# Two heads' keys and queries in the two halves of the array's rows: a causal attention with a routed expert layer, one core

## What is computed

```python
q = (x @ Wq).reshape(B, S, HEADS, HEAD_DIM).transpose(0, 2, 1, 3)     # 16 heads of 16
c_kv = x @ Wkv_down
k = (c_kv @ Wk_up)...; v = (c_kv @ Wv_up)...
qf = concat(q_nope, rope(q_rope)); kf = concat(k_nope, rope(k_rope))
scores = jnp.einsum('bhqd,bhkd->bhqk', qf, kf) * scale
scores = jnp.where(causal, -jnp.inf, scores)
weights = jax.nn.softmax(scores, axis=-1)
out = jnp.einsum('bhqk,bhkd->bhqd', weights, v)
```

## Time and profile before

| | us |
|---|---|
| median of three runs | 789.13 |
| the profiled execution | 787.88 |
| its span, first to last instruction | 786.1 |
| TensorE (matmul) busy | 699.7 |
| VectorE busy | 567.3 |
| ScalarE busy | 397.4 |

### The profile page before, as it was taken

One profiled execution on the slowest core, in us unless ns is written; L12 is line 12 of the kernel. 1 busy time (PEld: TensorE's weight loads), 2 busy tenths in 40 slices (PEclk: granted clock), 3 DMA queues, 4 the chain that ended last, 5 costly groups with the idle time before them and its releaser, 6 DMA issues.

```text
span 786.1 us, 13117 instructions
## 1 busy us (share of the span) xinstructions
PE 699.7 (89%) x4086; PEld 444.5 (57%) x4087; DVE 567.3 (72%) x1297; ACT 397.4 (51%) x848; POOL 240.3 (31%) x297
## 2 busy tenths in 40 slices
PE   3579899899999999999999999999979999999910
PEld 3456575565665556556654555554467777777710
DVE  6666679778879977787698888863687755555545
ACT  2225365455656666667666776766823232222204
POOL 6526173440072207010611000010147413333332
PEclk9759899899999999999999999999999999999965
DMA  4864315035015101500341265332332223333254
GB/s 138 204 172 109 83 43 148 24 103 119 1 42 148 56 1 41 121 2 1 93 89 65 65 215 189 126 97 57 87 98 102 90 83 95 108 108 108 87 187 160
DMA packets 45096, 75.94 MB, mean 97 GB/s; under 512 B 5695, under 2 KB 23359, under 8 KB 44863
## 3 DMA queue, kind: packets, MB, share of 16 engines
q1 hardware_dynamic: 37423, 57.55, 27.2%
q0 software_dynamic: 4896, 13.67, 5.0%
q10 hardware_dynamic: 2720, 4.00, 1.4%
HBM read 41.91 MB, written 32.93 MB: 95 GB/s over the span
## 4 chain that ended last, share of the span: by engine, by line
PE 70%; DVE 16%; DMA 4%; issue 4%; ACT 3%; ACTq 1%; POOL 0%; SPq 0%; POOLq 0%; DVEq 0%
PE banks_ps L1144 15%; PE banks_ps L1124 14%; PE banks_ps L1085 14%; PE banks_ps L1181 7%; DVE mx L1342 6%; PE banks_ps L1215 5%; PE banks_ps L1001 3%; PE banks_ps L1092 2%; PE banks_ps L1194 2%; DMA q_stack<-m_rows 2%; PE banks_ps L1228 1%; ACT probs L888 1%; PE banks_ps L1277 1%; PE banks_ps L1203 1%; DVE base L1809 1%
## 5 line engine op out<-in xcount | busy, mean ns | idle before, releaser
L1342 DVE TENSOR_REDUCE mx<-banks_ps 128x1 f32<-128x512 f32 (+3 forms) x640 | 346.6, 602 | 93.1 <-PE banks_ps L1085 50.1
L888 ACT ACTIVATE probs<-banks_ps 128x512 f32<-128x512 f32 (+3 forms) x640 | 304.1, 546 | 180.9 <-PE banks_ps L1124 166.6
L1124 PE MATMUL banks_ps<-q_stack,k_stack 98*128 98x512 f32 (+3 forms) x640 | 244.9, 399 | 15.5 <-ACT probs L888 7.2
L1085 PE MATMUL banks_ps<-k_stack,q_stack 96*128 96x512 f32 (+3 forms) x640 | 237.0, 400 | 7.3 <-DMA q_stack<-kq_split 3.4
L1085 PEld LDWEIGHTS banks_ps<-k_stack,q_stack 96*128 96x128 f32 x640 | 124.8, 198 | 82.0 <-DVE mx L1342 37.1
L1124 PEld LDWEIGHTS banks_ps<-q_stack,k_stack 98*128 98x128 f32 x640 | 122.4, 195 | 51.4 <-ACT probs L888 29.1
L741 POOL TENSOR_SCALAR_AFFINE_SELECT probs<-probs 128x512 f32<-128x512 f32 x64 | 41.0, 640 | 331.0 <-ACT probs L888 331.0
L1144 PE MATMUL banks_ps<-probs,v_ones 128*17 128x512 f32 (+3 forms) x1280 | 134.1, 536 | 1.0 <-POOL probs L741 1.0
L798 POOL DMA_INDIRECT token_y<-ys,dest x47 | 45.4, 966 | 79.2 <-DVE ys L1785 76.3
L1144 PEld LDWEIGHTS banks_ps<-probs,v_ones 128*17 128x17 f32 x1280 | 29.5, 97 | 64.9 <-issue 41.1
L1181 PE MATMUL banks_ps<-w_up_sb,xg_t 128*128 x188 | 63.8, 462 | 0.3 <-ACT xg_t L941 0.3
(11 more groups left out here) (186 smaller groups left out, 685.0 us busy)
## 6 DMA issues: line engine op xcount, KB each, us to landing
kq_split<-kq_stage SPq DMA_DIRECT2D x32, 256.0 KB, 3.4
k_stack<-kq_split SPq DMA_DIRECT2D x8, 768.0 KB, 6.6
q_stack<-kq_split SPq DMA_DIRECT2D x32, 192.0 KB, 6.1
xg<-slot_x SPq DMA_DIRECT2D x47, 130.0 KB, 2.1
slot_x<-blank SPq DMA_DIRECT2D x11, 520.0 KB, 6.9
w_up_sb<-w_up SPq DMA_DIRECT2D x16, 352.0 KB
kq_split<-kq_stage SPq DMA_DIRECT2D x32, 128.0 KB, 3.2
x_raw<-xT SPq DMA_DIRECT2D x4, 512.0 KB, 5.7
```

The costliest lines, as they stand in the source:

```text
L888: nc.scalar.activation(probs[:, s % PROB_BUFS, h, off:CH], score_bank(n)[:, off:CH], ACT.Exp)\
L1085: ins = nc.tensor.matmul(dst[:, at:at + keys], q_stack[0:STACK, u % 4, h, tile * P:(tile + 1) * P], k_stack[0:STACK, pair, kb * CH + k0:kb ...
L1124: nc.tensor.matmul(score_bank(n)[:, off:CH], k_stack[:, 2 * g + h // 2, b * P:(b + 1) * P], q_stack[:, u % 4, h, off:CH], start=True, stop ...
L1342: last = nc.vector.tensor_reduce(mx[:, u % 2, h * TPC + tile, kb:kb + 1], bank_of(bank)[:, at:at + keys], AX.X, ALU.max)
```

## The change

The even head of a pair now has rows 0 to 47 of `k_stack` and `q_stack`, the odd one rows 64 to 111, with two rows of ones or of maxima behind each (48 and 49, 112 and 113). `q_stack` has one slot for a pair, and no zeros. A matmul then reads 48 or 50 rows of one half of the array's rows instead of 96 or 98. The program's matmuls on such operands carry a tile of 64 rows by 128 columns, at row 0 or row 64; all others keep 128 by 128, or 128 by 32 for the values.

A turn for maxima is now a pair of banks: two matmuls one behind the other, for the two heads, then two masks where there are masks, one wait before them and one release after VectorE's two reductions. The four scores of a step are issued in two twos, behind the pair of banks instead of between single banks. The rotation of the four PSUM banks hands two to each pair. Keys are loaded by two DMAs instead of one.

```diff
+ROWS = SPLIT + 2
+HALF_ROWS = P // 2
...
-        filled.append(filled[-1] + BANKS_A_STEP[u // UNITS_PER_CHUNK])
+        filled.append(filled[-1] + BANKS_A_STEP[u // UNITS_PER_CHUNK] / 2)
...
     for n, turn in enumerate(turns):
-        bank = n % TURN_BANKS if n < first_alone else LAST_MAX_BANKS + n % 2
-        turn_bank[turn], turn_before[turn] = bank, user.get(bank)
-        user[bank] = turn
+        wide = 2 if turn in max_no else 1
+        turn_banks[turn] = [(at + k) % TURN_BANKS if n < first_alone else LAST_MAX_BANKS + at % 2 for k in range(wide)]
+        turn_before[turn] = [user.get(bank) for bank in turn_banks[turn]]
+        user.update((bank, turn) for bank in turn_banks[turn])
+        at += wide
...
-                    sp.dma_start(k_stack[0:STACK, 4 * m:4 * m + 4, c * CH:(c + 1) * CH].bitcast(F32),
-                                 kq_dram[c, n - 1].rearrange("two copy (d j) n -> (two copy d) j n", j=GH)).then_inc(k_stacked, 16)
+                    for par in range(2):
+                        sp.dma_start(k_stack[half_rows(par, SPLIT), 4 * m:4 * m + 4, c * CH:(c + 1) * CH].bitcast(F32),
+                                     kq_dram[c, n - 1, par].rearrange("copy (d j) n -> (copy d) j n", j=GH)).then_inc(k_stacked, 16)
...
                 for tile, k0, keys, at in parts:
-                    ins = nc.tensor.matmul(dst[:, at:at + keys], q_stack[0:STACK, u % 4, h, tile * P:(tile + 1) * P],
-                                           k_stack[0:STACK, pair, kb * CH + k0:kb * CH + k0 + keys],
+                    for par in range(2):
+                        ins = nc.tensor.matmul(bank_of(of, par)[:, at:at + keys],
+                                               q_stack[half_rows(par, SPLIT), u % 4, pair, tile * P:(tile + 1) * P],
+                                               k_stack[half_rows(par, SPLIT), stacked, kb * CH + k0:kb * CH + k0 + keys],
...
-                nc.tensor.matmul(score_bank(n)[:, off:CH], k_stack[:, 2 * g + h // 2, b * P:(b + 1) * P],
-                                 q_stack[:, u % 4, h, off:CH], start=True, stop=True).then_inc(pe_scores, 1)
+                nc.tensor.matmul(score_bank(n)[:, off:CH], k_stack[half_rows(h % 2), 2 * g + h // 2, b * P:(b + 1) * P],
+                                 q_stack[half_rows(h % 2), u % 4, h // 2, off:CH], start=True, stop=True).then_inc(pe_scores, 1)
...
                 for half in range(2):
-                    for h in (2 * half, 2 * half + 1):
-                        run_banks(banks[h])
-                        if s < NS:
-                            score_head(s, h)
+                    run_banks(banks[half])
+                    if s < NS:
+                        score_head(s, 2 * half)
+                        score_head(s, 2 * half + 1)
...
-            nc.vector.memset(q_stack[0:STACK, 2:4].bitcast(F32), 0.0).then_inc(zeros_high, 1)
...
+                for tile, _, keys, at in bank_parts(of):
+                    for par in range(2):
+                        n = mx_row_of(pair, par, tile)
+                        last = nc.vector.tensor_reduce(mx[:, u % 2, n, kb:kb + 1], bank_of(of, par)[:, at:at + keys], AX.X, ALU.max)
+                last.then_inc(max_done, 1)
```

More of the change, by code:

```diff
@@ L80, in build_program, with max_pairs, bank_parts @@
     first_step[UNITS] = len(steps)
-    def max_banks(u):
+    def max_pairs(u):
         c = u // UNITS_PER_CHUNK
-        return [(u, h, i, kb) for h in range(GH) for i in range(TPC) for kb in range(c)] + \
-               [(u, h, n, c) for h in range(GH) for n in range(len(OWN_BANKS))]
-    def bank_parts(bank):
-        u, h, n, kb = bank
+        return [(u, pair, i, kb) for pair in range(GH // 2) for i in range(TPC) for kb in range(c)] + \
+               [(u, pair, n, c) for pair in range(GH // 2) for n in range(len(OWN_BANKS))]
+    def bank_parts(pair_of_banks):
+        u, pair, n, kb = pair_of_banks
         if kb < u // UNITS_PER_CHUNK:
@@ L118, in build_program @@
         at = min(at, first_step[u] - MAX_AHEAD)
-        for bank in reversed(max_banks(u)):
+        for bank in reversed(max_pairs(u)):
             while at >= 0 and len(max_at[at]) >= room(at):
@@ L489, in score_bank, with bank_of, half_rows, mx_row_of @@
             return turn_ps[:, k - SCORE_BANKS]
-        def bank_of(turn):
-            return turn_ps[:, turn_bank[turn]]
+        def bank_of(turn, k=0):
+            return turn_ps[:, turn_banks[turn][k]]
+        def half_rows(par, rows=ROWS):
+            return slice(HALF_ROWS * par, HALF_ROWS * par + rows)
+        def mx_row_of(pair, par, tile):
+            return (par * (GH // 2) + pair) * TPC + tile
         def wait_read(eng, job):
@@ L960, in bank_free @@
             def bank_free(turn):
-                before = turn_before[turn]
-                if before in max_no:
-                    pe.wait_ge(max_done, max_no[before])
-                elif before:
-                    wait_read(pe, before)
+                for before in turn_before[turn]:
+                    if before in max_no:
+                        pe.wait_ge(max_done, max_no[before])
+                    elif before:
+                        wait_read(pe, before)
                 return bank_of(turn)
@@ L1331, in _, with reduce_pair @@
                                         ALU.subtract).then_inc(w_ready, 1)
-            def reduce_bank(bank):
-                u, h, i, kb = bank
-                c = u // UNITS_PER_CHUNK
-                n = max_no[bank]
-                if u >= 2 and bank == max_banks(u)[0]:
-                    dve.wait_ge(mx_ready, u - 1)
-                dve.wait_ge(pe_max, n)
-                for tile, _, keys, at in bank_parts(bank):
-                    last = nc.vector.tensor_reduce(mx[:, u % 2, h * TPC + tile, kb:kb + 1],
-                                                   bank_of(bank)[:, at:at + keys], AX.X, ALU.max)
+            def reduce_pair(of):
+                u, pair, i, kb = of
+                if u >= 2 and of == max_pairs(u)[0]:
+                    dve.wait_ge(mx_ready, u - 1)
+                dve.wait_ge(pe_max, max_no[of])
+                for tile, _, keys, at in bank_parts(of):
+                    for par in range(2):
+                        n = mx_row_of(pair, par, tile)
+                        last = nc.vector.tensor_reduce(mx[:, u % 2, n, kb:kb + 1], bank_of(of, par)[:, at:at + keys], AX.X, ALU.max)
                 last.then_inc(max_done, 1)
@@ L1669, in _ @@
             for s in range(NS + 1):
-                banks, jobs = quarters(max_at[s]), quarters(aux_at[s], 2)
-                for k in range(4):
-                    for bank in banks[k]:
-                        reduce_bank(bank)
-                    if k % 2:
-                        for job in jobs[k // 2]:
-                            if job in by_dve:
-                                read_aux(job)
-                    norm_part(s, k)
+                banks, jobs = quarters(max_at[s], 2), quarters(aux_at[s], 2)
+                for half in range(2):
+                    for bank in banks[half]:
+                        reduce_pair(bank)
+                    norm_part(s, 2 * half)
+                    for job in jobs[half]:
+                        if job in by_dve:
+                            read_aux(job)
+                    norm_part(s, 2 * half + 1)
                 for u in range(UNITS):
```

71 lines of the change are left out of this document (35 added, 36 removed).

## The result

The changed kernel takes 883.43 us (median of 4 runs, 881.68 to 884.77) where the kernel before takes 789.62 on the same chip (4 runs, 788.01 to 790.67): 1.1189 times, 95% interval 1.116 to 1.1217. The forecast was 782, with 0.36 on slower. Its profiled span is 883.0 us against 786.1. The ratios of this document leave out executions more than 1.5% above the fastest of their kernel, so where the times scatter a ratio is not that of the two medians.

What follows compares the result with a forecast made beforehand. TensorE's issue was taken as a narrow bound, VectorE next. Full steps -7, side jobs -9 and +6, own banks +2, start +2, last unit -1 sum to -7 us: 787.9 to 781 profiled, 782 median; range 762 to 806.

Steps and rivals of the forecast that it cites:

- What bounds the kernel: Before the change, TensorE's issue bounds full steps narrowly (5.72 of 5.76 us for two steps); VectorE is next.
- the chain of full steps: Off-diagonal steps with maxima: the wait moves to the two-pair buffer before VectorE; 0.17 us less per two steps, -7 us.
- Overlap of the halves: Two 512-column matmuls side by side in the array's halves take 0.24 us; bounds 0.235 (full overlap) and 0.47 (none).
- Rival C: No overlap: matmuls in two halves follow one another, a two costs 0.47 us; +18, 806 us; chance 0.12.
- Side jobs: 128 by 128 jobs beside maxima: odd steps absorb 0.5 us each, -9 us; even steps pay 0.2 each, +6 us.
- rival A: Tiling changes cost 0.6 us or more, not 0.4; pairs needing the pair just before idle VectorE; 800 us; chance 0.28.
- Own banks: Own banks and diagonal steps, bounded by TensorE: islands cost 0.4 us each, twos save 0.24; +2 us, bounds -10 to +30.
- the island: Mask at 128 rows between 64-row matmuls: tiling change out and back plus two weight loads, some 0.4 us.
- The start: Unit 0: queries load 0.5 us late, own pairs with masks make TensorE slower than VectorE by some 1.5 us; +2 us.
- A: In "A's price", rival A; in "idle gaps is A", the experiments' theory that the clock falls because TensorE works less of the time.
- the spoiler: Granted clock under 1.00 in units 8 to 15, the array being asked for less; no size or chance given.
- TensorE's busy time falls by tens of us: Sign that the forecast is right: TensorE's busy time falls by tens of us while the span hardly moves.

Runs made afterwards that it cites:

- run 2: Changed kernel with its pair order kept, but keys and queries stacked at full height (96 and 98 rows, zeros) as before: 847.73 us, 1.0605 times the kernel before.
- run 12: The changed kernel measured once more, nothing edited, beside the later experiments: 884.92 us, 1.1231 times the kernel before.
- run 3: Changed kernel with its half-height layout kept, but banks and scores issued singly in turns as before: 943.2 us, 1.1797 times the kernel before.
- run 10: Kernel before with only its operand rows edited, maxima and scores both over rows 0 to 63: 951.71 us, 1.2057 times the kernel before.

## Why the prediction was wrong

**What bounds the kernel; the chain of full steps: right.** 5.59 us was forecast for two full steps, 5.68 came: right in kind, but half of the forecast gain (0.08 us where 0.17 was added up). In the chain, pair 4 was to start 3.15 us after pair 1 and started 3.18 after; the next block was due at 3.75 and came at 3.84 (0.03 of the 0.09 is there already, and 0.07 is the way from the pair to its scores, 592.38 to 592.69, where 0.24 was counted; the way into the values, 0.35, is as forecast). TensorE's gain went into a wait for the two-pair buffer, as said: its weight loads wait 71.6 us for VectorE, 37.1 before.

**Overlap of the halves: right, at the upper bound.** 0.24 for a two. Rival C fell on this (its mark was blocks over 5.9); run 2 shows what it would have been: 6.34.

**Side jobs: wrong in sign at the full clock.** -3 us was forecast for all of them, with 0.5 gained wherever a job stands in an odd step. Seven of the 21 periods at the full clock have a side job beside maxima; each got longer, together from 45.42 to 48.90 us. In the second trace of the changed kernel (run 12) there are five, from 31.11 to 33.31. The period that starts at 357.59 us before and 425.65 after has two jobs and grew from 6.87 to 7.57: the pair behind the first job starts at 430.67, after an idle gap of 0.55 that VectorE ends, 3.18 after the first pair (427.49). That is when the second pair is reduced, not the first. The job had taken one of the four banks, so the pair behind it needed banks of the pair just before. This is a mechanism of rival A, which the sum left out.

**Own banks: right.** In the changed kernel:

```profile
435.07 0.50 PE L1096 MATMUL banks_ps<-k_stack,q_stack 48*128 48x512 f32 x2
435.50 0.28 PE L1105 MATMUL banks_ps<-mask_b,ident_b 128*128 128x128 bf16 x2
435.72 0.50 PE L1137 MATMUL banks_ps<-q_stack,k_stack 50*128 50x512 f32 x2
436.06 0.40 PE L1096 MATMUL banks_ps<-k_stack,q_stack 48*128 48x384 f32 x4
...
438.59 0.38 PE L1096 MATMUL banks_ps<-k_stack,q_stack 48*128 48x256 f32 x2 [0.53 <-DVE mx L1354]
```

From 435.07 to 436.06 are 0.99 us for a pair of own banks, two masks and two scores: 0.48 for the twos, 0.08 for the masks at the 0.04 of the earlier trace rows, so 0.43 for the island, where 0.4 was taken. The wait of 0.53 at 438.59 stands behind a side job, as above. Five periods at the full clock have own banks and no job; together they fell from 31.42 to 30.73 us (four in run 12, from 26.38 to 25.22).

**The start: right.** The first exponential starts at 54.2 us where it started at 52.7, 1.5 later; +2 was forecast.

**What the sum would have been at the full clock.** The four periods of full steps alone went from 23.54 to 24.02 us (run 12: 23.34 to 23.03), those of the last unit from 25.69 to 25.11. The 78 periods are 33 with jobs beside maxima, 13 with own banks alone, 24 of full steps and 8 of the last unit. With the change of each kind as the two traces give it, the stage would be 8 to 17 us longer at the full clock (an estimate; periods of one kind differ among themselves), nearly all by the side jobs: some 797 to 806 us, near rival A, and not 782. A's price in the prediction is itself not added up well: 782 and +15 to +30 have their middle at 804, not 800.

**The step that failed: the clock.** The prediction used the full clock for every duration of units 8 to 15, and its last sentence named the spoiler, "A granted clock under 1.00 in units 8 to 15 would spoil all of it, since the array is asked for less", without a price, a rival or a chance. It happened, in 57 of 78 periods. So the sign "TensorE's busy time falls by tens of us" came out the other way: it rose from 699.7 to 757.8 us, since the same matmuls took longer. The price can be read from one period that holds the same work in every kernel and is at the low level throughout or nearly so: 5.52 us in the kernel before at the full clock, 7.08 in the changed kernel, 7.83 in run 3, 9.58 in run 10. Overlap makes the low clock cheaper, but not free. Over the stage +96.0 us stand against 255.8 - 17.7 = 238.1 us more low clock, 0.40 us for each; without the 8 to 17 us of above it is 0.33 to 0.37, so 79 to 88 of the 96 us are the clock's (an estimate). The reason given in the prediction was also only half of it: "asked for less" by idle gaps is A, and run 10 had none of these gaps, only fewer rows, and 302 us of low clock. The 0.50 on faster came from rivals that all shared the one clock.

What stays open: whether it counts that a matmul is held in one half of the array or that it is under some height (only 48, 50, 64, 66 and more rows were run, and 66 only in the maxima), how far the time of going from one height to another lowers the clock, and whether both halves at work together count as a full array. Nor was the mask as two half-height matmuls tried.

## What to carry to other kernels

Before packing matmuls into halves of the array, price the case in which TensorE runs at the low clock for a third to a half of the stage: packing pays only where that loses less than the overlap gives, and a kernel held by another engine's buffer gives the overlap back anyway. When untouched instructions get longer (here the values, 536 to 696 ns), read the granted clock by stretch before any wait. Keep matmuls of 64 rows and fewer apart from taller ones: each change between the two cost 0.2 us at the full clock and 0.3 at the low one, while 96, 98 and 128 rows alternated at no such cost. And when a buffer is handed out in wider pieces, look at what else takes from it: here one bank for a side job made the next pair wait for the pair just before it.

## What the runs showed of the hardware that was not expected

- The granted clock went with the height of the matmuls: 66 rows in the maxima and 98 in the scores, 47 us at the low level; 64 rows in both, 302 us; with the same instructions in the same order and TensorE shown busy for 97% and 99% of the stage.
- A two of matmuls in the two halves takes 0.24 us at the full clock, the time of one (0.235); at that pace its weight loads lie beside the matmuls of the two before it (loads at 589.54 us, matmuls at 589.78).
- Maxima of 64 rows between scores of 98 made the kernel 1.43 times as long, with TensorE "busy" 94% of the span: the 0.2 to 0.3 us of each change are in the busy share.
- Of two orders at half height, singles in turns (run 3, 321 us of low clock) and twos (the changed kernel, 256), the one with more idle time had the better clock (TensorE busy 98% and 91% of the stage). Run 2 had idle gaps at full height (busy 92%) and 27 us.
